# A layer with a diagonal-block state space scan and a small gated network on Trainium2: the states' share of y by tiles of 32 rows and 128 columns

## The chip, the core and the metric

One NeuronCore of a Trainium2 chip runs one program. Its engines work side by side and meet at semaphores: TensorE (PE in the profile, its weight loads PEld), VectorE (DVE), ScalarE (ACT), GpSimd (POOL) and SyncE (SP), which issues most DMA transfers. The metric is the device time of one execution in microseconds, as the median of several runs. The profile is of one execution; its span is from the first to the last instruction.

## The reference, cut to what matters

The input is x with 8192 rows of 512 channels. The part of the kernel that matters here is a linear recurrence with 16 states in each channel:

```python
h = _layernorm(x, axis=-1) * (1 + ca) + sa
def step(h, x_t):
    h = jnp.einsum('dnm,bdm->bdn', A, h) + Bm[None] * x_t[..., None]
    y_t = jnp.einsum('dn,bdn->bd', Cm, h) + Dm * x_t
    return (h, y_t)
_, y = jax.lax.scan(step, h0, jnp.swapaxes(x, 0, 1))
```

Then come a layernorm of y, gelu, a 512x512 product, a gate and a residual, and behind them a second layernorm, a network with 64 inner columns of 16 hidden values each, and a second gated residual.

## The kernel before

**Tiling.** Time is cut into 64 chunks (NC) of 128 steps (L = P = 128). The 512 channels form 64 groups (NG) of 8 channels (GC); 8 channels of 16 states fill the 128 partitions, so partition 16c + n holds state n of channel c. The kernel works in two halves of 32 groups (HG) each.

**Stages of a half.** First the powers of the 16x16 matrices are built by doubling (lines 1172 and 1175), then the taps of the recurrence, the inputs of the chunks and a scan over the 64 chunks (line 1235), which leaves in PV the state at each chunk's start. Then comes the y loop, which the change touches: for each group, y is the sum of a share of the states and a Toeplitz product of the taps with the chunk's own inputs.

**The y loop on TensorE.** It goes over the 32 groups g, and before each fourth one stands a block of products for the four groups g to g+3, called a quad below. These are the states' share: WP[rows, group, 1:129], the output rows of each state for the 128 steps, is the stationary operand, and BDH the moving one. BDH holds the chunk states of a group with a mask, so that a partition of one channel is nonzero only in that channel's columns; a column block is 64 chunks wide. The eight channels of a group fill one PSUM bank of 512 columns. Before, a matmul takes 64 rows (4 channels, BW = 64) and 256 columns (4 channels by 64 chunks); a group needs two, one per half of the rows, into two halves of the same bank, and the two halves of the rows may not work on one bank at a time. The index h says which half; i is the pass (0 or 1), e the group within the quad. The bank of a group is t_bank(g) = (g + 2) % 6. In the second pass every other matmul waits, with o_mm, for the two of the first pass that wrote the same banks. Behind the quad the Toeplitz products of the four groups run (line 1283, 16 matmuls of 64 columns in each group, into the same banks).

**Who feeds it.** POOL writes BDH from PV with the mask par4 (line 470), in a ring of four groups (g % 4), and signals bdh_r; it waits with o_mm until the second-pass matmul that read the slot is done. Every 256 KB Toeplitz tile is loaded from DRAM by SP (line 331) into a ring of five, when the product five groups earlier is done (t_mm), and ScalarE copies one quarter of it (line 653) and signals tc_r. DVE evicts a finished group (line 833) and signals y_ev, which frees its bank. Toward the end of the first half POOL also makes two power blocks of the second half (line 408) between the masked states of groups 27 and 28. Other waits count o_mm too: POOL's memset of CM and ScalarE's first copy of the second half, and ScalarE's loads of W_out in the second y loop.

**After the loops** follow layernorm, transposes, the output product and the network over 32 units (lines 1301 to 1378), in which TensorE is the busiest engine as well.

Of the kernel before, what the change touches and what calls it, by code (L numbers as in the profile page):

```python
# [12 lines left out]
P = 128  # L13
# [3 lines left out]
L = P  # L17
NC = T // L
# [3 lines left out]
HG = NG // HALVES  # L22
# [5 lines left out]
H0 = L - NC  # L28
# [17 lines left out]
BR = 32  # L46
# [21 lines left out]
BDR = 4  # L68
BW = 4 * NS
# [3 lines left out]
def adaln_ssm_kernel(nc, x_in, A_in, Bm_in, Cm_in, Dm_in, lnw_in, lnb_in, Wo_in, bo_in,  # L73
# [3 lines left out]
    ALU = mybir.AluOpType  # L77
# [8 lines left out]
    with ctx:  # L86
# [30 lines left out]
        UR = C0[:, 4096:5120]  # L117
# [29 lines left out]
        BDH = UR.rearrange("p (r h c) -> p r h c", r=4, h=4)  # L147
# [74 lines left out]
        def t_bank(g):  # L222
            return (g + 2) % 6
# [143 lines left out]
        def _(gp):  # L367
# [44 lines left out]
            for half in range(HALVES):  # L412
                base = half * HSTEPS
                for n in range(AHEAD if half else 0, STEPS):
# [16 lines left out]
                    if n == STEPS - 2 + (half == 0):  # L431

                        if half == 0:
                            gp.wait_ge(S["bct_ev"], 1)
                            gp.wait_ge(S["xh_r"], NC)
                        else:
                            gp.wait_ge(S["o_mm"], 2 * half * HG)
# [26 lines left out]
                for g in range(HG):  # L464
# [3 lines left out]
                    if g >= 4:  # L468
                        gp.wait_ge(S["o_mm"], 8 * (n // 4 - 1) + 4 + n % 4 + 1)
                    gp.tensor_tensor(BDH[:, g % 4, :, 1:NC], PV[:, g, H0:H0 + NC - 1].unsqueeze(1).to_broadcast([P, 4, NC - 1]),  # L470
                                     par4[:, :].unsqueeze(2).to_broadcast([P, 4, NC - 1]), ALU.mult).then_inc(S["bdh_r"], 1)
# [66 lines left out]
        def _(act):  # L538
# [45 lines left out]
            def late_weights(g):  # L584
# [5 lines left out]
                if g in (7, 11, 15, 19):  # L590
                    o = (g - 7) // 4
                    act.wait_ge(S["o_mm"], 2 * HG + 8 * (o + 1))
                    act.dma_start(WoN[:, o, :], Wo_in[o * P:(o + 1) * P, :]).then_inc(S["ld_wo"], 16)
# [11 lines left out]
            for half in range(HALVES):  # L605
                base = half * HSTEPS
                if half:
                    act.wait_ge(S["o_mm"], 2 * half * HG)
                act.activation(WP[:, :, L], BCT[:, 64 + half * HG:64 + (half + 1) * HG], ACT.Copy).then_inc(S["w0_r"], 1)
                for n in range(STEPS):  # L610
# [8 lines left out]
                    if half and n == 0:  # L619
                        act.wait_ge(S["o_mm"], 2 * half * HG)  # L620
                        act.wait_ge(S["bdh_r"], half * HG)
# [485 lines left out]
        def _(pe):  # L1107
# [41 lines left out]
            for half in range(HALVES):  # L1149
# [90 lines left out]
                for g in range(HG):  # L1240
# [26 lines left out]
                    if g % 4 == 0:  # L1267
                        for k in range(8):
# [5 lines left out]
                            elif e % 2 == 0:  # L1274
                                pe.wait_ge(S["o_mm"], 2 * n + e + 2)
                            gi, h = g + e, (i + e) % 2
                            ci, ri = slice(256 * h, 256 * h + 256), slice(BW * h, BW * h + BW)
                            pe.matmul(PS[:, t_bank(gi), ci], WP[ri, gi, 1:L + 1], BDH[ri, gi % 4, :, :], start=(i == 0), stop=False,  # L1278
# [191 lines left out]
```

## Time and profile before

| | |
|---|---|
| median of 3 runs | 761.77 us (761.5 to 762.27) |
| span of the profiled execution | 763.1 us |
| TensorE busy | 706.2 us (93%) |
| DVE, ACT, POOL busy | 533.1, 470.9, 483.1 us |
| first y loop | 158.27 to 208.94 us |
| second y loop | 317.35 to 373.45 us |
| mean granted TensorE clock | 0.983 of 2.4 GHz |

The profiled execution's span is 1.3 us longer than the median of the timed runs. A float32 matmul appears as two records of weight load and two of matmul; a record's end is modelled, so records that overlap in time can be one stream that is back to back. Idle time of an engine that is not the bottleneck costs nothing.

### The profile page before, as it was taken

Reading aid. Unit: us, or ns where it says so; the run is one execution under the profiler, and the core shown is the slowest. Engines: PE = TensorE matmul, PEld = TensorE weight load, DVE = VectorE, ACT = ScalarE, POOL = GpSimd, SP = SyncE. Lnnn points to the kernel's source line nnn. Section 1 sums busy time; section 2 is a strip of 40 time slices with the busy share of each in tenths; the row PEclk is TensorE's granted clock in tenths of the full one; section 3 lists DMA queues with packets and bytes.
Section 4 is the critical chain, followed back from the end, with each engine's and each line's share of the span. In section 5 each row is a group of like instructions: output and inputs, shape, how many; then the busy total and the mean of one; then the engine's idle time right before and its main releaser. Section 6 shows DMA issues by size and latency. Waiting matters only on the chain.

```text
span 763.1 us, 24715 instructions
## 1 busy us (share of the span) xinstructions
PE 706.2 (93%) x10079; PEld 493.9 (65%) x10079; DVE 533.1 (70%) x1192; ACT 470.9 (62%) x1007; POOL 483.1 (63%) x684
## 2 busy tenths in 40 slices
PE   5797978899999898999699999999999999999997
PEld 4774867888899877887545555555455555555564
DVE  7886866844643468544734688788888888877776
ACT  1674966133322471244246888888988888888872
POOL 5664633743455507654288988788888888887710
PEclk9999999999999999999889999999999999999999
DMA  7977400259500002388423002322232232231114
GB/s 223 364 229 274 154 17 3 44 122 174 127 6 4 3 24 45 86 200 177 143 92 111 1 30 82 111 105 81 92 111 83 85 110 84 84 111 55 57 41 153
DMA packets 78209, 78.18 MB, mean 102 GB/s; under 512 B 16144, under 2 KB 49552, under 8 KB 78096
## 3 DMA queue, kind: packets, MB, share of 16 engines
q1 hardware_dynamic: 77072, 74.76, 32.6%
q10 hardware_dynamic: 1024, 1.84, 0.9%
q8 instruction: 80, 1.31, 0.7%
q14 instruction: 33, 0.27, 0.1%
HBM read 59.28 MB, written 17.30 MB: 100 GB/s over the span
## 4 chain that ended last, share of the span: by engine, by line
PE 49%; DVE 1%; POOL 0%; ACT 0%; DVEq 0%; issue 0%; ACTq 0%; POOLq 0%
PE PS L1309 30%; PE PS L1378 4%; PE PS L1356 4%; PE PS L1301 4%; PE PS L1343 4%; PE PS L1393 1%; PE PS L1319 1%; PE PS L1330 0%; ACT arenaC L664 0%; DVE ebs L979 0%; PE PS L1323 0%; DVE arenaC L995 0%; DVEq L86 0%; POOL sy L392 0%; DVE XY L833 0%
## 5 line engine op out<-in xcount | busy, mean ns | idle before, releaser
L1309 PE MATMUL PS<-arenaC,arenaA 128*128 128x512 f32 x512 | 242.0, 605 | 0.0
L408 POOL TENSOR_TENSOR arenaC<-arenaA,par 128x512 f32<-128x512 f32 x104 | 107.3, 1039 | 82.6 <-ACT arenaA L647 41.8
L1309 PEld LDWEIGHTS PS<-arenaC,arenaA 128*128 128x128 f32 x512 | 90.2, 191 | 87.6 <-issue 83.1
L1172 PE MATMUL PS<-arenaA,arenaC 64*64 64x80 f32 (+1 forms) x1792 | 116.4, 233 | 9.0 <-DVE arenaC L821 4.0
L700 ACT ACTIVATE arenaA<-PS,ffc 128x256 f32<-128x256 f32 x224 | 111.8, 578 | 12.3 <-PE PS L1356 12.3
L1175 PE MATMUL PS<-arenaA,arenaC 64*64 64x64 f32 (+1 forms) x1792 | 114.7, 218 | 2.3 <-issue 2.3
L1025 DVE SCALAR_TENSOR_TENSOR PS<-arenaA,ffc,PS 128x256 f32<-128x256 f32 x196 | 95.2, 486 | 22.3 <-ACT arenaA L700 5.7
L1172 PEld LDWEIGHTS PS<-arenaA,arenaC 64*64 64x64 f32 x1792 | 96.0, 138 | 15.6 <-issue 7.9
L821 DVE STREAM_TRANSPOSE arenaC<-arenaC 128x512 f32<-128x512 f32 x104 | 73.0, 705 | 43.1 <-POOL arenaC L408 35.9
L1175 PEld LDWEIGHTS PS<-arenaA,arenaC 64*64 64x64 f32 x1792 | 98.5, 137 | 2.8 <-issue 2.8
L672 ACT ACTIVATE arenaA<-PS,lnwb 128x256 f32<-128x256 f32 x128 | 65.8, 574 | 44.3 <-PE PS L1301 44.3
L506 POOL TENSOR_TENSOR ROWS<-ROWS 128x512 f32<-128x512 f32 x64 | 81.5, 1274 | 5.3
L833 DVE TENSOR_TENSOR XY<-PS,arenaA 128x256 f32<-128x256 f32 x128 | 48.2, 419 | 49.6 <-PE PS L1283 49.6
L653 ACT ACTIVATE arenaC<-arenaC 64x512 f32<-64x512 f32 x64 | 39.5, 628 | 59.7 <-DMA arenaC<-kernel_taps 59.4
L1283 PE MATMUL PS<-XY,arenaC 128*64 128x64 f32 x2048 | 68.4, 224 | 4.3 <-ACT arenaC L653 4.1
L1283 PEld LDWEIGHTS PS<-XY,arenaC 128*64 128x64 f32 x2048 | 64.4, 138 | 12.0 <-ACT arenaC L653 6.7
L1235 PE MATMUL PS<-arenaA,arenaC 64*64 64x80 f32 x1536 | 60.1, 231 | 8.8 <-DVE arenaA L1445 7.4
L1235 PEld LDWEIGHTS PS<-arenaA,arenaC 64*64 64x64 f32 x1536 | 56.4, 133 | 12.8 <-DVE arenaC L821 6.3
L470 POOL TENSOR_TENSOR arenaC<-arenaA,par 128x252 f32<-128x252 f32 x64 | 37.6, 618 | 40.9 <-PE PS L1278 40.9
L623 ACT ACTIVATE arenaA<-PS 128x128 f32<-128x128 f32 x56 | 15.8, 282 | 74.1 <-PE PS L1175 74.0
L1301 PEld LDWEIGHTS PS<-ident,arenaC 128*128 128x128 f32 x256 | 32.6, 143 | 40.1 <-issue 40.1
L664 ACT ACTIVATE arenaC<-XY,sy 128x512 f32<-128x512 f32 x64 | 49.5, 831 | 7.6 <-POOL sy L394 7.6
(198 smaller groups left out, 1252.3 us busy)
## 6 DMA issues: line engine op xcount, KB each, us to landing
arenaC<-kernel_taps SPq DMA_DIRECT2D x64, 256.0 KB, 4.7
XY<-in_L_attn_x SPq DMA_DIRECT2D x38, 256.0 KB, 5.6
arenaC<-in_L_attn_x SPq DMA_DIRECT2D x15, 512.0 KB, 3.6
out<-arenaC SPq DMA_DIRECT2D x15, 512.0 KB, 2.7
arenaC<-in_L_attn_x SPq DMA_DIRECT2D x26, 256.0 KB, 4.7
XY<-in_L_wmod SPq DMA_DIRECT2D x6, 1024.0 KB, 9.2
XY<-in_L_attn_x SPq DMA_DIRECT2D x11, 512.0 KB, 3.5
out<-XY SPq DMA_DIRECT2D x10, 512.0 KB, 2.8
```

The source lines that it names most:

```text
L408: gp.tensor_tensor(BDs[:, step % BDR, :, :].rearrange("p g (a m) -> p g a m", m=NS), src, msk, ALU.mult).then_inc(S["bdp_r"], 1)
L506: chain(gp.tensor_tensor(tmp, tmp, Grow, ALU.mult))
L672: act.activation(zT[:, u % 2, q, :].rearrange("p (t i) -> p t i", i=P), PS[:, b, (q % 2) * UW:(q % 2 + 1) * UW].rearrange("p (t i) -> p t ...
L700: act.activation(rr[:, h % RELU_RING, :], PS[:, bank, 0:FP * P], ACT.Relu, scale=W1c[:, h:h + 1], bias=b1c[:, h:h + 1]).then_inc(S["relu_r ...
L821: dve.transpose(BDTs[:, step % BDR, :, :], BDs[:, step % BDR, :, :]).then_inc(S["bdt_r"], 1)
L1025: ins = dve.scalar_tensor_tensor(out=dst, in0=rr[:, h % RELU_RING, :], scalar=W2c[:, h:h + 1], in1=g, op0=ALU.mult, op1=ALU.add)
L1172: pe.matmul(pv_ps(r)[e:e + BW, j, LW - nw:LW + NS], BDTs[e:e + BW, b, j, :], PV[e:e + BW, g, PW - nw:PW + NS], start=True, stop=True)
L1175: mm = pe.matmul(w_ps(r)[e:e + BW, j, LW - nw:LW], BDs[e:e + BW, b, j, :], WP[e:e + BW, g, L + 1 - nw:L + 1], start=True, stop=True)
L1235: mm = pe.matmul(pv_ps(n % 2)[e:e + BW, j, 0:NS + NC], BDTs[e:e + BW, n % BDR, j, :], PV[e:e + BW, g, H0:PW + NS], start=True, stop=True)
L1283: mm = pe.matmul(PS[a:a + 64, t_bank(g), h * NC:(h + 1) * NC], Tring[g % TR][:, h, a:a + 64], channel(n * GC + h), start=False, stop=(h == ...
L1301: mm = pe.transpose(PS[:, b, i:i + P], hatY[:, t, q * P:(q + 1) * P], ident[:, :])
L1309: mm = pe.matmul(PS[:, 2 + t, :], zT[:, u % 2, q, t * P:(t + 1) * P], WoT[:, q, :], start=False, stop=(q == QB - 1))
```

## The change

The states' share is cut in tiles of 32 rows (BR = 32, two channels) and 128 columns (two channels by 64 chunks). A group now needs four matmuls (OP = 4), and a quad 16 in four passes; in each pass the four groups stand in four different row tiles and four banks, h = (i + e) % 4. Every matmul of the passes 2 to 4 waits with o_mm for the one four places ahead, which wrote the same bank. The masked states cover two channels instead of four (mask par, 128x2x64), in the same memory, so the ring holds eight groups (HR = 8) instead of four, and POOL waits for the slot eight groups back. All other counts of o_mm are rewritten from 2 to OP per group.

```diff
+HR = 8
+OP = 4
-        BDH = UR.rearrange("p (r h c) -> p r h c", r=4, h=4)
+        BDH = UR.rearrange("p (r a c) -> p r a c", r=HR, a=2)
...
-                            gp.wait_ge(S["o_mm"], 2 * half * HG)
+                            gp.wait_ge(S["o_mm"], OP * half * HG)
...
-                    if g >= 4:
-                        gp.wait_ge(S["o_mm"], 8 * (n // 4 - 1) + 4 + n % 4 + 1)
-                    gp.tensor_tensor(BDH[:, g % 4, :, 1:NC], PV[:, g, H0:H0 + NC - 1].unsqueeze(1).to_broadcast([P, 4, NC - 1]),
-                                     par4[:, :].unsqueeze(2).to_broadcast([P, 4, NC - 1]), ALU.mult).then_inc(S["bdh_r"], 1)
+                    if g >= HR:
+                        gp.wait_ge(S["o_mm"], OP * 4 * ((n - HR) // 4) + 4 * (OP - 1) + n % 4 + 1)
+                    gp.tensor_tensor(BDH[:, g % HR, :, 1:NC], PV[:, g, H0:H0 + NC - 1].unsqueeze(1).to_broadcast([P, 2, NC - 1]),
+                                     par[:, :].unsqueeze(2).to_broadcast([P, 2, NC - 1]), ALU.mult).then_inc(S["bdh_r"], 1)
...
-                        for k in range(8):
+                        for k in range(4 * OP):
                             i, e = k // 4, k % 4
                             if i == 0 and e % 2 == 0:
                                 if g >= 4:
                                     pe.wait_ge(S["y_ev"], n + e - 4)
                                 pe.wait_ge(S["bdh_r"], n + e + 2)
-                            elif e % 2 == 0:
-                                pe.wait_ge(S["o_mm"], 2 * n + e + 2)
-                            gi, h = g + e, (i + e) % 2
-                            ci, ri = slice(256 * h, 256 * h + 256), slice(BW * h, BW * h + BW)
-                            pe.matmul(PS[:, t_bank(gi), ci], WP[ri, gi, 1:L + 1], BDH[ri, gi % 4, :, :], start=(i == 0), stop=False,
+                            elif i > 0:
+                                pe.wait_ge(S["o_mm"], OP * n + 4 * (i - 1) + e + 1)
+                            gi, h = g + e, (i + e) % 4
+                            ci, ri = slice(P * h, P * h + P), slice(BR * h, BR * h + BR)
+                            pe.matmul(PS[:, t_bank(gi), ci], WP[ri, gi, 1:L + 1], BDH[ri, gi % HR, :, :], start=(i == 0), stop=False,
                                           skip_group_check=True).then_inc(S["o_mm"], 1)
```

TensorE's queue at the first quad of the first half, before (line 1278 is the quad, 1283 the Toeplitz products of group 0; the names in brackets are the semaphores that an instruction waits for):

```order
573 L1278 MATMUL PS<-arenaC,arenaA 128x256 [waits tz_r,bdh_r,bz_r,scan_h]
574 L1278 MATMUL PS<-arenaC,arenaA 128x256
575 L1278 MATMUL PS<-arenaC,arenaA 128x256 [waits bdh_r]
576 L1278 MATMUL PS<-arenaC,arenaA 128x256
577 L1278 MATMUL PS<-arenaC,arenaA 128x256 [waits o_mm]
578 L1278 MATMUL PS<-arenaC,arenaA 128x256
579 L1278 MATMUL PS<-arenaC,arenaA 128x256 [waits o_mm]
580 L1278 MATMUL PS<-arenaC,arenaA 128x256
581 L1283 MATMUL PS<-XY,arenaC 64x64 [waits tc_r]
```

The same place on TensorE's queue with the change (its lines are two further down, 1280 and 1285):

```order
573 L1280 MATMUL PS<-arenaC,arenaA 128x128 [waits tz_r,bdh_r,bz_r,scan_h]
574 L1280 MATMUL PS<-arenaC,arenaA 128x128
575 L1280 MATMUL PS<-arenaC,arenaA 128x128 [waits bdh_r]
576 L1280 MATMUL PS<-arenaC,arenaA 128x128
577 L1280 MATMUL PS<-arenaC,arenaA 128x128 [waits o_mm] x12
578 L1285 MATMUL PS<-XY,arenaC 64x64 [waits tc_r]
```

Eight matmuls with two waits on o_mm have become 16 with twelve; nothing else has moved there.

POOL's queue from the masked states of the first groups on, before (line 470; 408 makes power blocks, 478 clears a part of a Toeplitz tile):

```order
113 L478 MEMSET arenaC 128x8x64 [waits lvl_mm]
114 L470 TENSOR_TENSOR arenaC<-arenaA,par4 128x4x63 [waits o_mm] x4
...
121 L408 TENSOR_TENSOR arenaC<-arenaA,par4 128x512 [waits lvl_mm,bdt_r,ld_A,v0_r]
122 L408 TENSOR_TENSOR arenaC<-arenaA,par4 128x512 [waits bdt_r,lvl_mm,ld_A]
123 L470 TENSOR_TENSOR arenaC<-arenaA,par4 128x4x63 [waits o_mm] x4
124 L408 TENSOR_TENSOR arenaC<-arenaA,par4 128x512 [waits lvl_mm,bdt_r,ld_A,t_mm]
```

The same stretch of POOL's queue with the change (line 472 makes the masked states, 410 the power blocks):

```order
113 L480 MEMSET arenaC 128x8x64 [waits lvl_mm]
114 L472 TENSOR_TENSOR arenaC<-arenaA,par 128x2x63 x4
...
121 L410 TENSOR_TENSOR arenaC<-arenaA,par4 128x512 [waits lvl_mm,bdt_r,ld_A,v0_r]
122 L410 TENSOR_TENSOR arenaC<-arenaA,par4 128x512 [waits bdt_r,lvl_mm,ld_A]
123 L472 TENSOR_TENSOR arenaC<-arenaA,par 128x2x63 [waits o_mm] x4
124 L410 TENSOR_TENSOR arenaC<-arenaA,par4 128x512 [waits lvl_mm,bdt_r,ld_A,t_mm]
```

The order is the same; the masked states of groups 4 to 7 no longer wait for the first quad, and each is half as wide.

## Rows read from the trace of the kernel before

**Rows 1.** The page: span, busy times, a costly group, a DMA issue.

```profile
span 763.1 us, 24715 instructions
...
PE 706.2 (93%) x10079; PEld 493.9 (65%) x10079; DVE 533.1 (70%) x1192; ACT 470.9 (62%) x1007; POOL 483.1 (63%) x684
...
L653 ACT ACTIVATE arenaC<-arenaC 64x512 f32<-64x512 f32 x64 | 39.5, 628 | 59.7 <-DMA arenaC<-kernel_taps 59.4
...
arenaC<-kernel_taps SPq DMA_DIRECT2D x64, 256.0 KB, 4.7
```

**Rows 2.** Windows: length, busy of PE, PEld, DVE, ACT, POOL, clock, DMA share.

```profile
158.27:208.94 50.67, 49.40 (x1155) 43.13 (x1155) 27.16 (x69) 19.60 (x33) 18.39 (x30) 1.00 0.72 154
317.35:373.45 56.10, 52.94 (x1184) 46.84 (x1184) 29.86 (x83) 23.24 (x38) 22.80 (x33) 0.97 0.71 167
...
352.00:355.50 3.50, 1.80 (x54) 1.52 (x50) 1.75 (x5) 1.25 (x2) 1.82 (x3) 1.00 0.96 188
355.50:358.90 3.40, 3.40 (x66) 3.28 (x62) 0.78 (x3) 3.02 (x5) 1.20 (x1) 0.50 0.57 133
```

**Rows 3.** Timeline of TensorE, first loop: start, us, line, records [idle before, releaser].

```profile
158.27 2.00 PE L1278 MATMUL PS<-arenaC,arenaA 64*128 64x256 f32 x16 [0.82 <-DVE arenaA L1445]
160.20 4.02 PE L1283 MATMUL PS<-XY,arenaC 128*64 128x64 f32 x128
...
202.62 0.70 PE L1278 MATMUL PS<-arenaC,arenaA 64*128 64x256 f32 x4
203.49 1.57 PE L1278 MATMUL PS<-arenaC,arenaA 64*128 64x256 f32 x12 [0.17 <-DVE XY L833]
204.99 4.02 PE L1283 MATMUL PS<-XY,arenaC 128*64 128x64 f32 x128
```

**Rows 4.** Timeline of TensorE, second loop.

```profile
355.29 3.54 PE L1283 MATMUL PS<-XY,arenaC 128*64 128x64 f32 x64 [0.72 <-ACT arenaC L653]
358.76 2.05 PE L1278 MATMUL PS<-arenaC,arenaA 64*128 64x256 f32 x16
360.74 1.16 PE L1283 MATMUL PS<-XY,arenaC 128*64 128x64 f32 x32
```

**Rows 5.** The first quad in narrow stretches of the timeline, and durations (min/median/max ns).

```profile
158.27 0.70 PE L1278 MATMUL PS<-arenaC,arenaA 64*128 64x256 f32 x4 [0.82 <-DVE arenaA L1445]
...
158.59 0.19 PEld L1278 LDWEIGHTS PS<-arenaC,arenaA 64*128 64x128 f32 x2
...
158.81 0.19 PEld L1278 LDWEIGHTS PS<-arenaC,arenaA 64*128 64x128 f32 x2
...
159.07 0.19 PEld L1278 LDWEIGHTS PS<-arenaC,arenaA 64*128 64x128 f32 x2
...
L1278 PE MATMUL PS<-arenaC,arenaA x2: 480/480/480, 158.3 to 158.3; 64*128 64x256 f32 x2
...
L1278 PE MATMUL PS<-arenaC,arenaA x256: 376/376/539, 158.3 to 368.4; 64*128 64x256 f32 x128
```

**Rows 6.** Timeline of TensorE behind the loops: biases from two row tiles.

```profile
427.76 0.39 PE L1319 MATMUL PS<-b1f,ones_bf 32*128 32x512 bf16 x1
427.76 0.38 PE L1323 MATMUL PS<-b1f,ones_bf 32*128 32x512 bf16 x1
```

**Rows 7.** Groups of TensorE by line and shape: busy us, mean ns of one.

```profile
L1343 PE MATMUL PS<-ident,arenaA 128*128 128x128 f32 x256 | 33.2, 273 | 0.0
...
L1211 PE MATMUL PS<-XY,arenaC 128*32 128x128 f32 x512 | 17.3, 276 | 1.7 <-ACT arenaC L633 1.4
```

**Rows 8.** Waits of the first loop, then of the second: us, times, longest.

```profile
PE PS L1283 <- ACT arenaC L653: 1.1, 3, 0.6
...
PE PS L1283 <- ACT arenaC L653: 3.0, 3, 1.3
```

**Rows 9.** Timeline of POOL at the first loop's last quad.

```profile
199.04 2.04 POOL L408 TENSOR_TENSOR arenaC<-arenaA,par 128x512 f32<-128x512 f32 x2 [5.01 <-DVE arenaA L798]
...
201.04 2.30 POOL L470 TENSOR_TENSOR arenaC<-arenaA,par 128x252 f32<-128x252 f32 x4
```

More of the change, by code:

```diff
@@ L591, in late_weights @@
                     o = (g - 7) // 4
-                    act.wait_ge(S["o_mm"], 2 * HG + 8 * (o + 1))
+                    act.wait_ge(S["o_mm"], OP * (HG + 4 * (o + 1)))
                     act.dma_start(WoN[:, o, :], Wo_in[o * P:(o + 1) * P, :]).then_inc(S["ld_wo"], 16)
@@ L607, in _ @@
                 if half:
-                    act.wait_ge(S["o_mm"], 2 * half * HG)
+                    act.wait_ge(S["o_mm"], OP * half * HG)
                 act.activation(WP[:, :, L], BCT[:, 64 + half * HG:64 + (half + 1) * HG], ACT.Copy).then_inc(S["w0_r"], 1)
@@ L619, in _ @@
                     if half and n == 0:
-                        act.wait_ge(S["o_mm"], 2 * half * HG)
+                        act.wait_ge(S["o_mm"], OP * half * HG)
                         act.wait_ge(S["bdh_r"], half * HG)
```

## The prediction

> **What bounds the kernel now.** I read the page's head first: TensorE is busy 706.2 of 763.1 us, every other engine 533.1 or less [rows 1]. A share like this only names the engine, so the next view is TensorE's own timeline in the two stretches that the change touches, the y loops of the two halves, 158.27 to 208.94 us and 317.35 to 373.45 us [rows 2]. There TensorE is busy 49.40 of 50.67 us and 52.94 of 56.10 us. Each stretch is eight rounds of the same thing: one "quad" (8 matmuls of line 1278, written as 16 records of 64x256, the states' share of y for four groups), then four groups of Toeplitz products (line 1283, 32 records each) [rows 3]. A quad starts at 158.27 and the products after it at 160.20, so a quad costs 1.93 us of TensorE; of the 16 quads 14 take this, one 2.37 (202.62 to 204.99) and one 1.98 (358.76 to 360.74) [rows 3, 4]. What the change does to the end of the program is what it does to these 16 numbers, less what TensorE's own waits in the loops swallow: behind the first loop TensorE goes on without a gap, and what follows the second one starts from its last product.
>
> Inside a quad the reader should see three things. Records come two by two: both row tiles of 64 rows load and stream together (the loads come x2). Rounds follow each other at 0.216 us (loads at 158.59 and 158.81), which is 256 columns twice at the 2.4 GHz level (0.213); the granted clock reads 1.00 there [rows 2, 5]. And the waits on o_mm cost next to nothing: the load that has one starts at 159.07, 0.26 us after the one before instead of 0.22, and its matmuls still follow on without a gap, because the other pair of banks is streaming meanwhile and the quad keeps its 1.93 us [rows 5].
>
> **What the change does to a quad.** Each matmul shrinks from 64 rows and 256 columns to 32 rows and 128 columns, and there are 16 of them in four rounds of four. Four row tiles of 32 rows stream at once. The columns streamed go from 4 x 2 x 0.213 = 1.71 us to 4 x 2 x 0.107 = 0.85 us, if four tiles really overlap. For the overlap the trace has two rows: 32-row bf16 matmuls in different row tiles start together at 427.76 [rows 6], and line 1211, four tiles by columns, takes 17.3 us for 512 records that last 276 ns each (34 ns per record, against 33.2 us for 256, or 130 ns, of line 1343 on the whole array) [rows 7]. So I take full overlap.
>
> But now every matmul of rounds 2 to 4 waits for the one four places ahead, the one that wrote the same bank, and nothing else is left to run: all four tiles are in the same round. Before, the wait looked back over a round that was still covered by another pair. So the latency of a matmul comes into the open three times a quad. From rows:
> the exposed weight load, 0.104 us (the quad's first two records last 480 ns, the others 376 [rows 5]); the first pass, 0.107 us; the second record, 0.273 us for 128 columns (line 1343) [rows 7]; from the end of a matmul to the load that waited for it, 0.09 us (the first two matmuls, four records, end at 158.27 + 0.70 = 158.97, the load comes at 159.07) [rows 5]. That is 0.104 + 0.107 + 0.273 + 0.09 = 0.574 us for a round, against the 2 x 0.216 = 0.43 us of a round before. A quad is then three such rounds and one without the last term, 3 x 0.574 + 0.484 = 2.21 us to its modelled end; the Toeplitz load starts 0.07 us before the modelled end (158.27 + 2.00 against 160.20 [rows 3]), which leaves 2.14 us. The row's 0.09 us stands behind two increments that come together; behind four it may be twice that (0.18 us, if they queue), and behind the one that a wait needs it may be half (0.045 us). These are the bounds, quads of 2.41 and 2.00 us; I take the row, rounded up to 2.15. Against 1.93 this is +0.22 us a quad, 16 x 0.22 = **+3.5 us** (bounds +1.1 and +7.7). Queued behind each of these waits on TensorE is the rest of the quad, then the four groups of products, and on those DVE's eviction (line 833) waits; DVE has room, so it only follows. The other waits on o_mm (ScalarE's copies and weight loads, POOL's memset for the next half) are rewritten to the same points and cost nothing.
>
> The Trainium skill bears on this twice. "TensorEngine Tiling (Array Packing)", section Restrictions and Gotchas, says that different row tiles cannot access one PSUM bank at the same time and that software must keep them apart; that is why the waits must stay, and the trace agrees in so far as the waits are in the program. "TensorE: Matmul & The Clock Gate", section on the per-tile semaphore tail, gives 25 + 4.7 per tile + 26.3 ns per increment, 149 ns for four; here the row shows 0.09 us behind two, about what it gives for two (87 ns). By it every restart comes after 0.15 us, the quad is 2.32 us and the 16 bring +6.2 instead of +3.5.
>
> **What the waits swallow.** Some Toeplitz groups already wait for their tile (ScalarE's copy, line 653, which waits for the load): three times in the first loop for 1.1 us in all, the longest 0.6, and three times in the second for 3.0 us, the longest 1.3 [rows 8]. A load is issued when the product five groups earlier is done, and between the two lies one quad. A stall is therefore shortened by one quad's lengthening, but only once along a chain of loads. Of these I count five that swallow 0.22 us each, **-1.1 us** (bounds 0 and -1.5, six of them in full plus some relief of the loads: the 16 DMA engines are 0.96 busy where the last of them stand, 352.00 to 355.50 [rows 2, 4]).
>
> **What POOL gives.** A masked-state product shrinks from 252 to 126 elements: 0.575 us (2.30 for four) to about 0.35, on the slope between 252 and 512 elements (0.575 and 1.02 us, 2.04 for two) [rows 9]. Where quads take their 1.93 us TensorE does not wait for them. One place counts. Behind the two power-block products at 199.04 POOL makes the last four masked states until 203.34, and the third and fourth matmul of the quad at 202.62 need the last two: TensorE resumes at 203.49 and the quad takes 2.37 us [rows 3, 9]. The profile names DVE L833 as the releaser, but the POOL row ends 0.1 us before. With the short ones all four are there by 201.04 + 1.4 = 202.44, before the quad begins. That is **-0.44 us**. The ring of eight costs nothing and is not needed elsewhere. The quad at 358.76 took 1.98 at a lower clock; not counted.
>
> **The sum.** 3.5 - 1.1 - 0.4 = +2.0 us. On the profiled execution that is 763.1 + 2.0 = 765.1 us of span; the span stands 1.3 us above the median of the timed runs, 761.77, so the time is 761.8 + 2.0 = **763.8 us**, its own range 763.0 to 765.5.
>
> **Rivals.**
> *The waits are cheaper than I read them, or the stalls swallow more.* With the lower bound the quads bring +1.1, of which five stalls swallow 0.07 each, and the sum is 1.1 - 0.4 - 0.4 = +0.3; with the forecast's quads and 1.5 us or a little more swallowed it is about +1.2. That is 762.1 to 763.0 us, no difference to be told; the runs shown spread from 761.5 to 762.27, so I let it begin at 761.2. For it: DMA engines at 0.96 have no room, and a slower TensorE lets them catch up. Against: the 0.09 us are a row. 0.31.
> *The gain comes.* If the weight loads and the next round are not held by the chain (the tiles drift apart and cover each other), a quad is four times 0.216 plus 0.2 = 1.07 us, 0.86 less, 16 x 0.86 = 13.8 us. The Toeplitz loads would then bind: between a load's issue and its use lie four groups and one quad, 4.0 + 1.1 = 5.1 us, and it takes 4.7 us at the median and 0.63 of copy [rows 1], more while the DMA engines are full. I let half be given back (an estimate): -7 us, 755 us. For it: half the streaming. Against: the waits are in program order on one queue, and a load that waits is seen to start only after what it waits for has ended. 0.1.
> *The increments queue.* The upper bound, quads of 2.41 us: +7.7 - 1.5 - 0.4 = +5.8 us, 767.6 us. For it: four matmuls now end at once where two did. Against: a wait needs one increment, not four, and may come before the other three. 0.06. (By the tail that the Trainium skill gives in "TensorE: Matmul & The Clock Gate" it would be +6.2 - 1.5 - 0.4 = +4.3 us, 766.1 us.)
> *The clock falls once more.* From 355.50 to 358.90 TensorE runs at 0.50 (the 1.2 GHz level), after 3.5 us in which it was busy 1.80; 64 records took 3.54 us there, against 4.02 us for 128, or 2.01 for 64, behind the first quad [rows 2 to 4]. That is 1.5 us for a fall. A quad whose tiles stream 0.85 of 2.15 us is thinner work, and where one meets a stall the clock may fall again. It decides against the change from one fall on: 763.8 + 1.5 = 765.3 us. Against: over the whole of the first loop, with its quads and three stalls [rows 8], the clock stayed at 1.00 [rows 2]. 0.09.
>
> **How the numbers follow.** Forecast 0.44, and the rivals 0.31, 0.1, 0.06, 0.09. The measurement can tell about 0.2% (1.5 us) from no change, that is 760.2 to 763.3. Of the forecast's own 0.44 about 0.06 lies below 763.3; slower 0.38 + 0.06 + 0.09 = 0.53, same 0.31 + 0.06 = 0.37, faster 0.10. The range from 761.2 to 766.2 leaves out the gain (0.10) and the queueing increments (0.06), and little more.
>
> **What would show it.** In the trace of after: the quad's 32 records and the distance from its first to the next Toeplitz load (2.15 expected; under 1.93 and I am wrong); loads of line 1280 in four bursts about 0.57 us apart; the stalls of TensorE shorter by about 0.2 us; no wait in the last quad of the first half; POOL's masked states at about 0.35 us each. A quad near 1.1 us would say that the latency is hidden; one of 2.15 us with an unchanged time that the loads bind.

## The result, and the profile of the changed kernel

The change makes the kernel slower: 765.44 us (median of 20 runs, 762.54 to 770.11) against 761.63 us (20 runs, 758.87 to 766.16), a ratio of 1.0051 (95% interval 1.0034 to 1.0068), which is 2.6 to 5.2 us. The forecast was 763.8 in a range of 761.2 to 766.2, slower with a chance of 0.53. The direction is right and the time is in the range, but twice the 2.0 us of the sum have come. Single executions of either kernel spread over 7 us, so one execution says little about 4 us; the traces are read below for what happens inside the loops. Every ratio below is of a kernel to the kernel before on the same chip.

The page of the changed kernel (its lines stand two further down: 1280 is the quad, 1285 the Toeplitz products, 655 ScalarE's copy), against [rows 1]:

```profile
span 765.1 us, 25227 instructions
PE 712.6 (93%) x10335; PEld 500.1 (65%) x10335; DVE 532.9 (70%) x1192; ACT 471.5 (62%) x1007; POOL 470.0 (61%) x684
L1285 PE MATMUL PS<-XY,arenaC 128*64 128x64 f32 x2048 | 70.4, 229 | 0.3 <-ACT arenaC L655 0.2
```

TensorE has 6.4 us more to do, POOL 13.1 us less (64 masked states of half the width), and DVE and ScalarE the same. The products of line 1285 wait for ScalarE's copy for 0.2 us in all. The timeline of TensorE, and under it that of its weight loads in the first quad (start, us, engine, line, records, idle before and releaser), answers to [rows 3, 5]:

```profile
157.34 2.23 PE L1280 MATMUL PS<-arenaC,arenaA 32*128 32x128 f32 x32 [0.82 <-DVE arenaA L1447]
159.51 5.53 PE L1285 MATMUL PS<-XY,arenaC 128*64 128x64 f32 x128
...
203.77 2.24 PE L1280 MATMUL PS<-arenaC,arenaA 32*128 32x128 f32 x32
```

```profile
157.34 0.31 PEld L1280 LDWEIGHTS PS<-arenaC,arenaA 32*128 32x128 f32 x8 [0.98 <-DVE arenaA L1447]
157.88 1.50 PEld L1280 LDWEIGHTS PS<-arenaC,arenaA 32*128 32x128 f32 x24 [0.23 <-PE PS L1280]
```

A quad begins at 157.34 and the products at 159.51: 2.17 us where 1.93 stood. The loads of the second pass start 0.54 us after those of the first (157.88). Of the 16 quads 14 take 2.16 or 2.17 us, and two meet a lower clock (2.28, and 2.56 at 346.14). The last quad of the first half (203.77) has no wait in it, where [rows 3] had 2.37 us with one. The products at 159.51 need 5.53 us for 128 records, where 4.02 is the rule: that is the clock. Windows of the changed kernel's loops, then around the falls in them (length, busy of PE, PEld, DVE, ACT, POOL, clock, DMA share), against [rows 2]:

```profile
157.34:209.67 52.33, 51.86 (x1279) 45.70 (x1281) 27.02 (x69) 19.61 (x33) 11.97 (x30) 0.97 0.65 149
318.32:374.87 56.55, 55.57 (x1309) 49.30 (x1311) 29.52 (x82) 23.32 (x38) 16.24 (x33) 0.94 0.70 166
...
156.50:159.90 3.40, 2.54 (x45) 1.97 (x46) 0.42 (x1) 2.47 (x5) 2.25 (x6) 1.00 0.37 88
159.90:163.30 3.40, 3.40 (x71) 3.40 (x68) 1.11 (x4) 0.63 (x1) 1.16 (x4) 0.50 0.21 59
317.00:320.30 3.30, 2.44 (x47) 1.84 (x42) 0.56 (x2) 2.46 (x5) 1.95 (x5) 1.00 0.62 186
320.30:323.70 3.40, 3.40 (x66) 3.18 (x62) 0.76 (x2) 0.00 (x0) 1.45 (x2) 0.50 0.47 127
344.20:347.60 3.40, 2.77 (x60) 2.42 (x55) 1.70 (x6) 1.19 (x2) 0.00 (x0) 1.00 1.05 218
347.60:351.00 3.40, 3.40 (x57) 3.05 (x53) 0.28 (x1) 2.38 (x4) 1.46 (x4) 0.50 0.65 136
```

In the loops TensorE is idle for 0.47 + 0.98 = 1.5 us; before it was 1.27 + 3.16 = 4.4 us [rows 2]. The clock was granted at the 1.2 GHz level three times (159.90, 320.30, 347.60), once before [rows 2]. Two of the three stand behind the first quad of a loop, ahead of which TensorE waits 0.82 us for the scan.

### The profile page after: what moved, and what is told of

The parts are those of the page before. It is cut to its first block, busy times and chain, and to the rows that moved or that the text cites. A ratio compares the mean times of both kernels' runs of the same rounds, so it can differ in the third digit from the quotient of the medians.

```text
span 765.1 us, 25227 instructions
## 1 busy us (share of the span) xinstructions
PE 712.6 (93%) x10335; PEld 500.1 (65%) x10335; DVE 532.9 (70%) x1192; ACT 471.5 (62%) x1007; POOL 470.0 (61%) x684
## 4 chain that ended last, share of the span: by engine, by line
PE 49%; DVE 1%; POOL 0%; ACT 0%; DVEq 0%; issue 0%; ACTq 0%; POOLq 0%
PE PS L1311 30%; PE PS L1380 4%; PE PS L1358 4%; PE PS L1303 4%; PE PS L1345 4%; PE PS L1395 1%; PE PS L1321 1%; PE PS L1332 0%; ACT arenaC L666 0%; DVE ebs L981 0%; PE PS L1325 0%; DVE arenaC L997 0%; DVEq L88 0%; POOL sy L394 0%; DVE XY L835 0%
## 5 line engine op out<-in xcount | busy, mean ns | idle before, releaser
L1285 PE MATMUL PS<-XY,arenaC 128*64 128x64 f32 x2048 | 70.4, 229 | 0.3 <-ACT arenaC L655 0.2
L1285 PEld LDWEIGHTS PS<-XY,arenaC 128*64 128x64 f32 x2048 | 67.0, 143 | 4.3 <-ACT arenaC L655 1.8
L625 ACT ACTIVATE arenaA<-PS 128x128 f32<-128x128 f32 x56 | 15.8, 282 | 72.2 <-PE PS L1177 72.1
L649 ACT ACTIVATE arenaA<-PS 128x128 f32<-128x128 f32 x48 | 13.3, 278 | 53.9 <-PE PS L1237 53.9
```

The costliest lines, as they stand in the source:

```text
L1285: mm = pe.matmul(PS[a:a + 64, t_bank(g), h * NC:(h + 1) * NC], Tring[g % TR][:, h, a:a + 64], channel(n * GC + h), start=False, stop=(h == ...
```

## The experiments

All numbers of a loop below run from its first quad to the last Toeplitz load; the loops' length is the sum of both. By this measure the kernel before has 50.46 + 55.83 = 106.3 us, and the change 52.33 + 56.55 = 108.9 us.

**Both kernels once more.** The change unchanged, and the kernel before for a second trace.

> The changed kernel once more, beside the kernel before on the same chip, for more pairs of times and for the granted clock of every run. Theory 1 (the quad's open latency alone): quads of 2.16 us against 1.93, time +2 us, mean clocks of the two kernels alike. Theory 2 (thinner quads let the clock fall more often as well): time +3 to +5 us and a lower mean clock, by about 0.0022 for each further fall of 3.4 us, each worth about 1.5 us.

> The kernel before once more, for its profile: quads of 1.93 us (one 2.37). The stalls for tile copies in the loops were 6.0 us and one clock fall in the profile that the prediction used; if that profile was a typical one they are 5 to 6 us again, if not, 3 to 4.

The change took 765.51 us (6 runs) against 761.74 (17 runs), ratio 1.0049 (1.003 to 1.0068). The time and the lower mean clock (0.9847 against 0.9885) are those of theory 2; whether its cause is the right one is taken up below. Of the change, the windows of the two loops, and the waits of TensorE's matmuls that bear on this (us, times, longest), in the first loop and then in the second:

```profile
157.94:209.79 51.85, 50.70 (x1280) 44.38 (x1282) 27.02 (x69) 19.54 (x33) 11.97 (x30) 1.00 0.68 150
318.45:374.62 56.17, 54.21 (x1310) 48.11 (x1312) 29.53 (x82) 23.32 (x38) 16.23 (x33) 0.97 0.71 167
```

```profile
PE PS L1285 <- issue: 0.7, 2, 0.4
...
PE PS L1259 <- issue: 0.7, 1, 0.7
PE PS L1285 <- issue: 0.6, 1, 0.6
...
PE PS L1285 <- ACT arenaC L655: 0.3, 1, 0.3
```

The same of the kernel before, a second execution:

```profile
155.48:206.25 50.77, 49.19 (x1151) 43.05 (x1153) 27.01 (x69) 19.52 (x33) 18.43 (x30) 1.00 0.74 153
315.40:369.78 54.38, 52.13 (x1181) 45.87 (x1183) 30.08 (x82) 23.29 (x38) 22.84 (x33) 1.00 0.76 172
```

```profile
PE PS L1283 <- ACT arenaC L653: 1.3, 3, 0.8
...
PE PS L1283 <- ACT arenaC L653: 1.6, 3, 0.8
...
PE PS L1283 <- issue: 0.6, 1, 0.6
```

The loops are 108.0 us against 105.2, 2.9 us more (2.6 in the first pair of traces). That is TensorE busy 104.91 against 101.32 us, +3.6, and idle 3.1 against 3.8 us, -0.7. The waits for ScalarE's copy, 2.9 us of before (4.1 in [rows 8]), have shrunk to 0.3 us (0.2 in the change's other trace). What has grown is "issue", idle time for which no semaphore accounts: 1.3 us ahead of products and 0.7 us in the small products of line 1259, 2.0 us in all (0.6 in the change's other trace), against 0.6 us in this trace of before and 0.2 us in the first. The last section shows what these pauses go with. The 2.9 us of the second trace of before are near the lower of the two ranges that were expected for it (3 to 4 us), though the 6.0 us put down there to the first trace stand in no row of the matmuls, which give 4.1. The rest of the program is the same to some tenths: from the end of the first loop to the start of the second 108.7 us in both traces of the change and 108.6 and 109.2 in those of before, and 389.1 to 390.3 us from the last load on. What differs most between single executions is the start of the first loop, 153.5 to 159.2 us over all traces here. The loops vary too: in the experiment on POOL below, which leaves TensorE's work in the loops as it was, they are 104.2 us, or 104.7 with the 0.44 us that it saves in a quad. Before is thus 104.7 to 106.3 us in three traces, the change 108.0 and 108.9 in two.

**Without the waits: each group its own row tile.** The row tile follows from the group (e) and not from pass and group, so a bank is written by one row tile and no wait is needed. The states' share then takes wrong rows of the operands; everything else is computed.

```diff
-                            elif i > 0:
-                                pe.wait_ge(S["o_mm"], OP * n + 4 * (i - 1) + e + 1)
                             gi, h = g + e, (i + e) % 4
-                            ci, ri = slice(P * h, P * h + P), slice(BR * h, BR * h + BR)
+                            ci, ri = slice(P * h, P * h + P), slice(BR * e, BR * e + BR)
```

> As the change, but in all four passes a group of the quad stays in its own row tile (rows and moving rows 32e instead of 32h), so that no two row tiles write one bank and the 12 waits of a quad are gone; the states' share of y is computed from the wrong rows, all else is the same work. If the open latency makes the quad (theory 1), it falls from 2.16 to about 1.08 us (4 x 0.216 and 0.2). If four row tiles do not overlap, it stays near 1.9. The time tells what the Toeplitz loads allow: 16 x 0.86 = 13.8 us under the kernel before if nothing binds, about -7 us if half is given back to stalls for the tile copies, unchanged if the loads bind fully.

757.28 us (6 runs), ratio 0.9945 (0.9923 to 0.9966). Timeline of TensorE:

```profile
154.66 1.17 PE L1278 MATMUL PS<-arenaC,arenaA 32*128 32x128 f32 x32 [0.82 <-DVE arenaA L1445]
155.77 3.99 PE L1283 MATMUL PS<-XY,arenaC 128*64 128x64 f32 x128
```

The same 16 matmuls take 1.11 us (15 quads at 1.10, one 1.48). So four row tiles do overlap in full, and the change's other 1.06 us a quad, 17 us in all, are its waits. Of the quads' 13.3 us against before the loops keep 98.5 against 105.2 to 106.3, 7 to 8 us, and the median time 4.5; the traced execution, at 754.36 us, is 2.9 us under that median.

**Quads of the change's length without its waits.** To the kernel before two matmuls of the identity by itself are added behind each quad (64 rows, 128 columns), into the banks of its third and fourth group, so y is not the reference's.

```diff
+                        for e in (2, 3):
+                            gi, h = g + e, (1 + e) % 2
+                            ci, ri = slice(256 * h, 256 * h + 128), slice(BW * h, BW * h + BW)
+                            pe.matmul(PS[:, t_bank(gi), ci], ident[ri, :], ident[ri, :], start=False, stop=False,
+                                      skip_group_check=True)
```

> The kernel before with two more matmuls of 64 rows and 128 columns at each quad's end (identity on identity, added into y, so y is off): the quad grows by 0.216 us to 2.14, about as much as by the change, but with TensorE streaming all the time, and POOL is as before. Theory 1: the same time as the change or 0.4 us more, +2 to +2.4 us. Theory 2: less than the change by the clock falls that it is spared, +1.5 to +2.5 us where the change has +4, and a mean clock like that of the kernel before.

764.27 us (12 runs), ratio 1.0028 (1.0006 to 1.0049): +2.5 us for 3.3 us of quads (15 at 2.15, one 2.37). The loops take 52.18 + 54.83 = 107.0 us, with no fall of the clock in them. The copy is still waited for (1.4 us in four waits and 0.8 us in one). By the median times a quad's length by itself thus swallows about one microsecond, near what was forecast, by the loops 1.4 to 2.6 us, and it may bring most of the change's cost. The interval is too wide to tell +2.5 from the change's +3.8.

**The wait bare in the kernel before.** The order of its eight matmuls: both passes of groups 0 and 1, then those of 2 and 3. Each wait now looks back at the pass just before, with no other pair of banks to cover it. POOL's count for a free slot is set to match the new order (not shown).

```diff
-                            i, e = k // 4, k % 4
+                            i, e = (k // 2) % 2, 2 * (k // 4) + k % 2
...
-                                pe.wait_ge(S["o_mm"], 2 * n + e + 2)
+                                pe.wait_ge(S["o_mm"], 2 * n + 2 * e + 2)
```

> The kernel before with the matmuls of a quad in another order: both passes of groups 0 and 1, then both of groups 2 and 3. The same 8 matmuls of 64 rows and 256 columns; but now the wait of a second pass looks back at the two matmuls right before it. Theory 1: two open latencies of 0.163 + 0.09 + 0.104 = 0.36 us, the quad is 1.93 + 0.71 = 2.64 us, 16 quads +11.3 us, less 1 to 4 us in the stalls: +7 to +10 us. Rival (a wait costs nothing, it is the row tiles of 32 that are slow): quads stay near 1.93 and the time the same.

769.59 us (5 runs), ratio 1.0107 (1.0082 to 1.0132). The weight loads of the first quad:

```profile
157.15 0.30 PEld L1278 LDWEIGHTS PS<-arenaC,arenaA 64*128 64x128 f32 x4 [0.99 <-DVE arenaA L1445]
157.94 0.73 PEld L1278 LDWEIGHTS PS<-arenaC,arenaA 64*128 64x128 f32 x8 [0.49 <-PE PS L1278]
...
159.18 0.30 PEld L1278 LDWEIGHTS PS<-arenaC,arenaA 64*128 64x128 f32 x4 [0.50 <-PE PS L1278]
159.81 0.32 PEld L1283 LDWEIGHTS PS<-XY,arenaC 128*64 128x64 f32 x8 [0.33 <-issue]
```

Every quad takes 2.66 us: two bare waits cost 2.66 - 1.93 = 0.73 us, 0.37 each. This is the mechanism of the change shown in the kernel before: not the wait, but that nothing else is left to run beside it. The quads are 11.3 us longer, the time 7.9.

**All four, or one for all.** The change with its first matmul of a pass waiting for the whole pass before:

```diff
-                            elif i > 0:
-                                pe.wait_ge(S["o_mm"], OP * n + 4 * (i - 1) + e + 1)
+                            elif i > 0 and e == 0:
+                                pe.wait_ge(S["o_mm"], OP * n + 4 * i)
```

> The change, but the first matmul of a pass waits for all four of the pass before and the other three wait for nothing (3 waits a quad instead of 12). If the four increments are handed out one after the other, about 0.043 us apart as the loads of the change restart, a pass waits 0.13 us longer: 0.67 us a pass, a quad of 3 x 0.67 + 0.41 = 2.42 us, 16 x 0.26 = +4.1 us over the change before stalls swallow some, so +2 to +4 us over it. If the number of waits is what costs, the quad gets shorter than 2.16.

And the same with a single increment, at the fourth matmul of a pass (all other counts of o_mm divided by four):

```diff
+                            elif i > 0 and e == 0:
+                                pe.wait_ge(S["o_mm"], OP * (n // 4) + i)
...
+                            mm = pe.matmul(PS[:, t_bank(gi), ci], WP[ri, gi, 1:L + 1], BDH[ri, gi % HR, :, :], start=(i == 0), stop=False,
+                                           skip_group_check=True)
+                            if e == 3:
+                                mm.then_inc(S["o_mm"], 1)
```

> The change, with one semaphore increment per pass of a quad (at its fourth matmul) instead of four, and one wait per pass (at its first matmul, for the whole pass before) instead of four. Measured so far: with four increments and four waits a quad takes 2.165 us and its loads restart every 0.542 us; with four increments and one wait for all four, 2.44 us. If the increments queue behind each other at 0.04 us apiece (theory), the single one arrives as early as the first of four does now: restart about 0.51 to 0.54 us, quad 2.05 to 2.2 us, and the time is that of the change within 1 us (764.5 to 766). Rival: the fourth matmul of a pass ends later than the first for another reason than the increments (issue), and the restart comes as late as with the wait for all four: quad 2.4 us or more, 766.5 us or more.

The loads of the first quad, of the one and of the other:

```profile
153.46 0.31 PEld L1280 LDWEIGHTS PS<-arenaC,arenaA 32*128 32x128 f32 x8 [0.98 <-DVE arenaA L1447]
154.13 0.31 PEld L1280 LDWEIGHTS PS<-arenaC,arenaA 32*128 32x128 f32 x8 [0.36 <-PE PS L1280]
...
155.90 2.20 PEld L1285 LDWEIGHTS PS<-XY,arenaC 128*64 128x64 f32 x72
```

```profile
156.39 0.31 PEld L1280 LDWEIGHTS PS<-arenaC,arenaA 32*128 32x128 f32 x8 [0.98 <-DVE arenaA L1449]
156.98 0.31 PEld L1280 LDWEIGHTS PS<-arenaC,arenaA 32*128 32x128 f32 x8 [0.28 <-PE PS L1280]
...
158.60 0.32 PEld L1287 LDWEIGHTS PS<-XY,arenaC 128*64 128x64 f32 x8
```

A pass restarts after 0.67 us with four increments and one wait for all (quads of 2.44 us), after 0.59 us with one increment (2.21 us), and after 0.54 us in the change (2.17 us). The times are 766.69 us (11 runs), ratio 1.0057 (1.0039 to 1.0076), and 764.76 us (12 runs), ratio 1.005 (1.0033 to 1.0068) on another chip. So increments do queue, 0.08 us for three of them, but the change's waits need the first of them only: four waits staggered behind four increments are as good as one of each. The single increment came a little later than its theory gave (0.59 us where 0.51 to 0.54 was put, a quad of 2.21 where 2.05 to 2.2 was), far from its rival's 2.4, and the time as that theory said. Of the 0.05 us by which it restarts later than the first of four, 0.02 are there because the fourth matmul of a pass starts 0.02 us after the first; the rest is not settled. The time of the wait for all four was missed: +2 to +4 us over the change was expected, and although its quads are 4.6 us longer in all than those of the change's second trace, and its loops 111.1 us against 108.0 and 108.9, the ratios 1.0057 and 1.005 can't be told apart.

**POOL's part alone.** The kernel before with POOL's two power blocks behind the last four masked states instead of ahead of them:

```diff
-                    if half == 0 and g == HG - 5:
+                    if half == 0 and g == HG - 1:
```

> The kernel before with POOL's two power blocks of the second half behind the last four masked states instead of ahead of them; nothing else. By the step on POOL the last quad of the first half falls from 2.37 to 1.93 us (-0.44 us), which is less than the times can show (same, within 0.2%); the trace decides. If it is DVE's eviction that the quad waits for, as the profile names it, the quad stays at 2.37.

762.43 us (12 runs), ratio 0.9992 (0.9972 to 1.0012). The last quad of the first half, POOL and TensorE:

```profile
200.07 2.30 POOL L470 TENSOR_TENSOR arenaC<-arenaA,par 128x252 f32<-128x252 f32 x4 [4.40 <-PE PS L1278]
...
204.29 2.00 PE L1278 MATMUL PS<-arenaC,arenaA 64*128 64x256 f32 x16
206.22 2.49 PE L1283 MATMUL PS<-XY,arenaC 128*64 128x64 f32 x76
```

The masked states are there at 202.37, the quad at 204.29 takes 1.93 us and the quads' sum falls from 31.3 to 30.8 us. So it was POOL that held the 2.37 us quad, and not DVE as the releaser says [rows 3]. The 0.44 us are visible in the quad and too small for the time.

**A bank of its own for each row tile.** This one computes y: the waits go because the layout needs none. The four banks of a quad no longer stand for its four groups but for four "units": unit h takes channels 2h and 2h+1 of each group. Row tile h then writes bank h alone, in four passes, one for each group. The Toeplitz tiles must follow that order; four transfers in DRAM per half make a second table of the taps (unit_taps) in the order of the units, so that a tile remains one load of 256 KB. DVE's eviction and the operand of the products take the channels by the same order.

```diff
-                            i, e = k // 4, k % 4
...
-                            elif i > 0:
-                                pe.wait_ge(S["o_mm"], OP * n + 4 * (i - 1) + e + 1)
-                            gi, h = g + e, (i + e) % 4
-                            ci, ri = slice(P * h, P * h + P), slice(BR * h, BR * h + BR)
-                            pe.matmul(PS[:, t_bank(gi), ci], WP[ri, gi, 1:L + 1], BDH[ri, gi % HR, :, :], start=(i == 0), stop=False,
+                            e, h = k // 4, k % 4
...
+                            ci, ri = slice(P * e, P * e + P), slice(BR * h, BR * h + BR)
+                            pe.matmul(PS[:, t_bank(g + h), ci], WP[ri, g + e, 1:L + 1], BDH[ri, (g + e) % HR, :, :], start=(e == 0), stop=False,
...
-                            mm = pe.matmul(PS[a:a + 64, t_bank(g), h * NC:(h + 1) * NC], Tring[g % TR][:, h, a:a + 64], channel(n * GC + h),
+                            mm = pe.matmul(PS[a:a + 64, t_bank(g), h * NC:(h + 1) * NC], Tring[g % TR][:, h, a:a + 64], channel(chan(n, h)),
```

> A version meant to keep the result and lose the waits: a PSUM bank takes the same two channels of four groups (one row tile) instead of eight channels of one group, so that a row tile always writes its own bank; Toeplitz tiles, products and evictions go by the same units, the taps are put in that order by four more transfers of 64 KB in each half. Quads of 1.10 us as in the run with own row tiles, 0.83 less than before. Latency theory: the time of that run, 757.3 us, -4 us against the kernel before (half of the 13.3 us lost to stalls for the tile copies), at most 1 us more for the longer way of the taps. If the taps come late, the first quad of a half starts later and it is worse than -4 by that.

> The kernel with one bank per row tile once more, on this chip beside the kernel before. The first run gave 755.1 us, ratio 0.9909 (0.9883 to 0.9936) and quads of 1.10 us. Theory: the quads are 1.10 us again in all 16 and the time 754 to 757 us. Rival: the first run profited from the chip; then the ratio lies above 0.9936. Open is whether the pauses of TensorE without a semaphore before it (7.2 us in the first trace) come again: if they belong to this kernel they are again over 4 us, if by chance under 2.

755.1 us (6 runs) against 761.66 (22 runs), ratio 0.9909 (0.9883 to 0.9936), and on another chip 755.9 (6 runs) against 760.93 (17 runs), ratio 0.9931 (0.9911 to 0.9951). This is the fastest kernel here, 5 to 7 us under the one before. The first time is 2.2 us better than the 757.3 us expected; the second is in its range, and its ratio is not above the bound that would have spoken for luck with the chip. Of the first run, timeline and windows:

```profile
156.41 1.17 PE L1285 MATMUL PS<-arenaC,arenaA 32*128 32x128 f32 x32 [0.82 <-DVE arenaA L1452]
157.52 3.99 PE L1290 MATMUL PS<-XY,arenaC 128*64 128x64 f32 x128
...
320.34 2.45 PE L1290 MATMUL PS<-XY,arenaC 128*64 128x64 f32 x75
324.24 1.77 PE L1290 MATMUL PS<-XY,arenaC 128*64 128x64 f32 x53 [1.44 <-issue]
```

```profile
156.41:204.79 48.38, 43.73 (x1280) 40.17 (x1282) 27.00 (x69) 19.59 (x33) 11.90 (x30) 1.00 0.73 161
313.75:363.70 49.95, 46.01 (x1309) 42.50 (x1311) 29.49 (x82) 23.35 (x38) 16.22 (x33) 1.00 0.80 188
```

Quads of 1.11 us (two of 1.15 and 1.17 in the second trace) save 13.6 us of TensorE; the loops are 98.3 us in both traces (105.2 to 106.3 before), and TensorE is idle 8.6 of them (3.8 to 4.4 before). Of that idle time 3.5 and 3.7 us are waits for ScalarE's copy, thus for the tiles' loads, and 5.0 and 4.4 us are "issue" in the middle of a group, whose tile is there (the 7.2 us in the expectation of the second run are not in the matmuls' rows). Both are over 4 us, and the kernel with a row tile for each group has 3.1 us, so it was no chance. The group of the products in section 5 of either page:

```profile
L1290 PE MATMUL PS<-XY,arenaC 128*64 128x64 f32 x2048 | 69.8, 223 | 8.6 <-issue 5.0
```

```profile
L1290 PE MATMUL PS<-XY,arenaC 128*64 128x64 f32 x2048 | 69.7, 223 | 8.6 <-issue 4.4
```

## Why the prediction was right, and where its sizes were off

**A quad, forecast 2.15 us: it takes 2.165.** The chain of load, two passes and restart was read rightly, and so was the overlap of four tiles. The restart was put at 0.57 us a round and is 0.54. By "TensorE: Matmul & The Clock Gate" of the Trainium skill, in its section on the per-tile semaphore tail, the quad would have been 2.32 us, an estimate with its 26.3 ns for each increment. The two runs with one wait for a pass show 0.08 us for three increments, 0.027 each, so the size of an increment agrees; the sum did not, because each wait needs its own increment and not the last.

**The gain, a rival at 0.1: rightly put low.** The waits are there because two row tiles must not write one bank together; "TensorEngine Tiling (Array Packing)" of the Trainium skill says so under Restrictions and Gotchas, and no run here breaks the rule. The kernel with a bank for each row tile obeys the same rule with no wait and has quads of 1.11 us, which was the price in the rival of the gain (1.07 us, half given back, 755 us). That rival's arithmetic fits a kernel that had to be written otherwise: 755.1 and 755.9 us were measured for it.

**POOL, -0.44 us: right**, in the change (no wait at 203.77; four masked states in 1.46 us where 1.4 was put) and alone. Only a reading is off: POOL's row ends 0.15 us before TensorE resumes, not 0.1.

**What the waits swallow, forecast -1.1 us (bounds 0 and -1.5): mis-sized.** The matmuls' waits for the copy went from 4.1 and 2.9 us in the two traces of before to 0.2 and 0.3, so 2.6 to 3.9 us were swallowed. The step counted one quad's lengthening once along a chain of loads. For quads that are longer and nothing else it was near the one microsecond that the identity products swallow by the median times. But whatever lengthens the loop gives the loads time, the clock's falls and the pauses below too: in the second trace of the change 3.3 us of quads, a fall of some 1.5 us and 1.4 us of pauses are 6.2 us, of which the loops show 2.9; in the kernel with bare waits 11.3 us of quads became 5.5 to 6.6 us of loops. About half is swallowed in these loops as long as there are stalls; by the median times it is less, 3.4 of the 11.3 us. That the DMA engines catch up is argued from their share, which falls from 0.74 and 0.76 to 0.68 and 0.71 in the second pair of windows; no run changed the loads alone.

**What is late next, not in the sum.** "Issue", without a semaphore, is 0.6 and 2.0 us in the loops of the change against 0.2 and 0.6 before, so it adds 0.4 and 1.4 us. A stall that goes leaves the next limit to be seen; the forecast's bounds had only the copy.

**The clock, a rival at 0.09 with 1.5 us a fall: seen in traces, not shown for the median.** In the loops the traces of the change have three falls and one, those of its two variants with one wait for a pass one each; five traces with quads of 64 rows have one, in [rows 2 to 4], and else none. Four of those six falls stand behind the first quad of a loop (of eight such places), in none of the ten of the kernels with 64 rows. The three kernels whose quads take 1.11 us (six such places) have no fall in their loops either.

The mean clock of the timed runs does not settle it. For the change it is 0.9847 against 0.9885 of the kernel before on the same chip, and one fall of 3.4 us lowers a mean by 0.5 x 3.4 / 765 = 0.0022. But the kernel with a row tile for each group has 0.9853 on that chip, with no fall in its traced loops, and the variant with one wait for all four has 0.9873 against 0.9874, with one. Falls stand outside the loops as well: every trace has a stretch of 6.8 or 10.2 us at the lower level right behind the second loop, and one to three falls ahead of the first. So a fall behind a quad whose tiles stream less than half of it costs its trace about 1.5 us, as the rival said, and the rival's argument against it (the first loop of before stayed at 1.00) did not carry over to the changed quads; how much of the 3.8 us in the median is the clock is not shown.

**The sum again.** The quads bring +3.8 us in the first pair of traces (31.3 to 35.1 us, 0.5 of it the lower clock) and +3.3 in the second, POOL's share in it; waits swallowed are -3.9 and -2.6; falls of the clock, 1.5 each, are two more in the first pair (+2.5 beyond what stands in the quads) and one in the second; issue is +0.4 and +1.4. That makes +2.8 and +3.6 where the loops measure +2.6 and +2.9. The time lies 2.6 to 5.2 us higher, so nothing outside the loops is needed. All that is not a quad, taken together, went from 74.95 and 73.86 us to 73.74 and 73.38, that is -1.2 and -0.5 us, near the -1.1 of the forecast. That is luck: two errors of opposite sign nearly cancel, too little swallowed, and the pauses and the clock left out.

**The profiled execution.** In the profiled executions here the time is the span and 1.7 to 1.8 us; the 763.1 us of [rows 1] thus belong to an execution of some 764.9 us, 3 us above the median. The step that set span against median let this pass as +1.3. It costs the sum nothing, since only a difference was carried over, but that trace had more waits for the copy (4.1 us against 2.9) and a fall of the clock that the second trace of before has not.

## What to carry to other kernels

Cutting a matmul into smaller row tiles halves its streaming only if the next pass doesn't wait for this one: count what else is left to run beside each wait, and put a bare one at load, passes and restart, here 0.54 us for 128 columns. If tiles of different rows must not share a bank, change which outputs share a bank before adding waits; the same matmuls took 1.11 us instead of 2.17. And when a stage's engine and its loads are both near full, expect to keep a third to half of what you take from the engine (here 4.5 to 6.6 of 13.5 us), and look for the next limit, such as the instructions' own transfers, and for the clock in the stretches where work gets thinner.

## What the runs showed of the hardware

A wait for the matmul just before on 64 rows and 256 columns costs 0.37 us when it is bare, next to nothing when another pair of banks is streaming.

TensorE pauses for up to 1.6 us in the middle of a group of products with no semaphore to wait for. In the kernel with a bank for each row tile one such pause ends at 324.24; windows before and in it, and the DMA queues from 320 to 324 us:

```profile
320.80:322.80 2.00, 2.00 (x67) 1.87 (x64) 1.07 (x3) 0.83 (x2) 1.98 (x2) 1.00 1.02 199
322.80:324.20 1.40, 0.00 (x0) 0.00 (x0) 0.44 (x2) 0.43 (x1) 1.34 (x4) 1.00 0.96 271
```

```profile
q8 instruction: 1, 0.02, 2.0%
```

The DMA engines are full, and one packet of instructions is among theirs. Where the pauses stand says more. TensorE in the same kernel's second trace:

```profile
317.61 0.83 PE L1290 MATMUL PS<-XY,arenaC 128*64 128x64 f32 x20 [1.62 <-issue]
318.37 1.17 PE L1285 MATMUL PS<-arenaC,arenaA 32*128 32x128 f32 x32
319.48 2.45 PE L1290 MATMUL PS<-XY,arenaC 128*64 128x64 f32 x75
322.26 1.75 PE L1290 MATMUL PS<-XY,arenaC 128*64 128x64 f32 x53 [0.34 <-issue]
323.94 1.17 PE L1285 MATMUL PS<-arenaC,arenaA 32*128 32x128 f32 x32
325.04 1.50 PE L1290 MATMUL PS<-XY,arenaC 128*64 128x64 f32 x43
327.10 2.76 PE L1290 MATMUL PS<-XY,arenaC 128*64 128x64 f32 x85 [0.55 <-issue]
```

From pause to pause it is 20 + 32 + 75 = 127 matmul records, then 53 + 32 + 43 = 128. This program has 82 packets of 16 KB on that queue for 10335 matmul records, one for 126. And each pause ends nearly the same time after such a packet: the packets before these three end at 316.17, 320.72 and 325.51 us, the pauses 1.44, 1.54 and 1.59 us later. Over the twelve traces there are 30 pauses of TensorE without a semaphore (over 0.15 us, from 150 to 390 us), those at line 1259 among them, and all 30 end 1.2 to 1.7 us after the end of a packet of this queue; of all matmul records of the loops about one in ten starts at that distance. So TensorE most likely waits in them for its next instructions. This is read from where the pauses stand; no run moved the packets. What stays open is why a packet comes late: the packets themselves take no longer in the loops than behind them (medians of 1.1 to 1.3 against 1.0 to 1.3 us).
